# Expert blocks from two tables: 41 blocks start on batches 0 to 5, batch 7 is routed among them

## What is computed

```python
x = x + attention(layernorm(x))           # uv = silu(xn @ uv_w.T); rope; squared relu of the scores
h = layernorm(x)                          # then, in the expert part:
xn = layernorm(h) * gamma + beta
probs = softmax(xn @ Wr + br);  scores, idx = top_k(probs, 2)
full[e] = relu(xn @ W1[e] + b1[e]) @ W2[e] + b2[e]
c = einsum('ef,efh->eh', relu(b1), W2) + b2;   c_total = c.sum(axis=0)
out = x + h + sum_k scores[k] * (full[idx[k]] - c[idx[k]] + c_total)
```

## Time and profile before

| | us |
|---|---|
| three executions | 404.68, 396.47, 397.13 |
| median | 397.13 |
| the profiled execution, its own time | 393.24 |
| its span, first to last instruction | 390.9 |
| TensorE busy, of the span | 319.3 (82%) |
| VectorE, ScalarE, GpSimd busy | 263.2, 240.2, 194.6 |

### The profile page before, as it was taken

The page is one execution under the profiler, slowest core; times in us unless marked ns, Lnnn a source line. Parts: engine busy times, 40 slices in busy tenths (PEclk is TensorE's granted clock), DMA queues, the critical chain, the costliest instruction groups (busy, mean ns, idle before and its releaser), DMA issues.

```text
span 390.9 us, 7957 instructions
## 1 busy us (share of the span) xinstructions
PE 319.3 (82%) x2031; PEld 258.5 (66%) x2031; DVE 263.2 (67%) x923; ACT 240.2 (61%) x466; POOL 194.6 (50%) x194
## 2 busy tenths in 40 slices
PE   2639999999999999999750599999999998999100
PEld 1525565666566666665650499999999998999000
DVE  4593598878788887772648377667767665776082
ACT  2656698888979797935030467667777776775000
POOL 4132060477667766575577035455555545555252
PEclk9987999999999999999995599999999999999655
DMA  7882200010100000010113212222222222221296
GB/s 177 285 231 82 90 0 0 3 37 17 43 15 29 28 28 27 23 34 20 37 48 102 69 35 69 63 67 78 69 63 73 71 70 70 58 61 50 90 356 199
DMA packets 33647, 29.01 MB, mean 74 GB/s; under 512 B 5393, under 2 KB 28980, under 8 KB 33604
## 3 DMA queue, kind: packets, MB, share of 16 engines
q1 hardware_dynamic: 24770, 18.33, 16.5%
q0 software_dynamic: 4352, 8.47, 6.6%
q10 hardware_dynamic: 4482, 1.72, 1.6%
HBM read 17.34 MB, written 11.68 MB: 74 GB/s over the span
## 4 chain that ended last, share of the span: by engine, by line
PE 59%; DVE 11%; ACT 9%; DMA 7%; issue 6%; POOL 4%; SPq 2%; ACTq 0%; POOLq 0%; DVEq 0%
PE B_uv L793 14%; PE B_o L806 14%; PE B_o L704 7%; PE B_S L688 6%; PE B_o L713 4%; PE B_S L692 3%; DMA W2s<-y 3%; ACT xs L499 3%; POOL slots L427 2%; DVE go L937 2%; DMA y<-u,xb 2%; PE B_uv L671 2%; PE B_uv L647 2%; DMA xb<-slots 2%; SPq L363 1%
## 5 line engine op out<-in xcount | busy, mean ns | idle before, releaser
L447 POOL DMA_INDIRECT y<-u,xb x72 | 70.4, 978 | 79.6 <-ACT u L601 75.3
L427 POOL DMA_INDIRECT slots<-rows,pos x64 | 65.2, 1019 | 30.7 <-issue 17.0
L806 PE MATMUL B_o<-W2s,K 128*128 x576 | 76.9, 276 | 0.4 <-DVE K L1105 0.4
L806 PEld LDWEIGHTS B_o<-W2s,K 128*128 128x128 f32 x576 | 70.1, 192 | 0.9 <-issue 0.6
L704 PE MATMUL B_o<-K,v 128*128 128x512 f32 x128 | 59.0, 594 | 0.0
L1105 DVE TENSOR_SCALAR K<-B_uv,t 128x128 f32<-128x128 f32 x144 | 40.6, 345 | 25.4 <-PE B_uv L793 25.4
L596 ACT ACTIVATE t<-W1s 128x644 f32 x36 | 26.7, 741 | 34.6 <-DVE yd L1100 18.8
L793 PE MATMUL B_uv<-xbT,t 128*128 128x128 f32 x288 | 39.9, 284 | 0.0
L793 PEld LDWEIGHTS B_uv<-xbT,t 128*128 128x128 f32 x288 | 36.7, 200 | 0.2 <-issue 0.2
L704 PEld LDWEIGHTS B_o<-K,v 128*128 128x128 f32 x128 | 23.0, 190 | 20.3 <-issue 19.1
L688 PE MATMUL B_S<-qk 128*128 128x512 f32 x64 | 34.2, 618 | 0.0
(11 more groups left out here) (166 smaller groups left out, 660.1 us busy)
## 6 DMA issues: line engine op xcount, KB each, us to landing
xb<-slots SPq DMA_DIRECT2D x72, 65.0 KB, 1.8
x_all<-L_attn_x SPq DMA_DIRECT2D x8, 256.0 KB, 3.6
W1s<-L_ffn_W SPq DMA_DIRECT2D x1, 2048.0 KB, 13.6
W1s<-y SPq DMA_DIRECT2D x4, 512.0 KB, 5.7
W2s<-y SPq DMA_DIRECT2D x4, 512.0 KB, 9.5
out<-acc ACTq DMA_DIRECT2D x5, 256.0 KB, 5.3
y<-u,xb POOLq DMA_INDIRECT x72, 2.2
slots<-rows,pos POOLq DMA_INDIRECT x64, 2.4
```

The source lines that it names most:

```text
L427: pool.indirect_dma_start(out=slots, out_offset=bass.IndirectOffsetOnAxis(ap=pos[:, q % 2, c:c + 1], axis=0), in_=rows[:, q % 2, k, t, :], ...
L447: pool.indirect_dma_start(out=y2, out_offset=bass.IndirectOffsetOnAxis(ap=xb[:, k, D:D + 1].bitcast(u32), axis=0), in_=yb[:, k, :], in_off ...
L806: last = nc.tensor.matmul(B_y[(m - 1) % 2], hT[:, (m - 1) % 2, c * P:(c + 1) * P], W2s[:, bass.ds(w + c * D, D)], start=(c == 0), stop=(c ...
```

## The change

The list of blocks is cut in two. Batches 0 to 5 have 6144 rows in 8 regions; 41 of their 128-row blocks are full whatever the routing, and they get a table of their own (`table_a`) while stage 7, the attention of the last batch, still runs. The 30 blocks of a second table (`table_b`) hold the rest, first that of batches 0 to 5 (14 blocks), then that of batches 6 and 7. In particular:

- The pipeline ends with stage 7. `prefix(r)` stands ahead of `output(a)`, and `positions(r)` behind `ln2_stats(a)`, in the same stage.
- On TensorE the sum of the counts of batches 0 to 5 stands in the attention of batch 7 and the first two blocks are transposed ahead of `output(7)`. Batch 7's `transpose_xn`, `router`, `prefix` and the second count stand in the block loop behind blocks 3, 5, 8 and 10 (`XN_AT` to `COUNT_AT`), and the parts of the other engines at the places that answer to them; `table_b` is spread over seven blocks of VectorE from block 11.
- GpSimd scatters batch 6 ahead of all `put`s, and batch 7 in 8 pieces behind `put(12)` to `put(19)`. SP zeroes all 8 tails ahead of load 32.
- `expert_constants` is replaced. The relu is `max(h, -b1)`, one VectorE instruction of 512 elements in place of 4 of 128, and what it leaves out, `b1 @ W2`, is folded into the constant row. The sums over b1 are 32 products with 9 columns (`constant_rows`) in stage -1, one copy, 8 small products (`constants_of`) and two ACT evacuations (`evac_d`) in stage 0. They need masks in SBUF (`eye8`, `own`), which GpSimd makes at the program's start; `own` is 17 partitions of 1024 elements. W2 is loaded from ACT's queue, ahead of ACT's first computation, and b2 as 8 rows.
- `xb` and `yb` have 16 slots in place of 8, and there are 71 blocks in place of 72.
- The sums of batches 0 to 5 are made in the block loop from block 61, one instruction a block, from loads that begin when block 54 is written; batches 6 and 7 are loaded after the last block in halves of 256 KB, summed by VectorE alone and stored in halves.

```diff
@@ constants @@
-NSLOT = 8
-NBLK = -(-(ROWS * TOPK // P + NE - 1) // NSLOT) * NSLOT
+NSLOT = 16
+OLD = 6
+FULL = OLD * L * TOPK // P
+NA = FULL - (NE - 1)
+NB1 = ((FULL - NA) * P + NE * (P - 1)) // P
+NBLK = ROWS * TOPK // P + NE - 1
+NB = NBLK - NA
+XN_AT, ROUTER_AT, EXP_AT, PREFIX_AT, COUNT_AT = 3, 5, 7, 8, 10
+SCATTER_AT, TAILS_AT, ADD_AT = 12, 32, 61
@@ SP @@
+            sp.wait_ge(tabA_step, TABA)
+            sp.wait_ge(scattered[0], 16 * TOPK * T * (OLD // 2))
+            sp.wait_ge(scattered[1], 16 * TOPK * T * (OLD // 2))
+            for n in range(NBLK):
+                if n >= NSLOT:
                     sp.wait_ge(y_ready, n - NSLOT + 1)
+                    sp.wait_ge(blk_stored[n % NSLOT], 16 * (n // NSLOT))
+                if n == TAILS_AT:
+                    sp.wait_ge(tabB_step, TAIL_AT)
+                    zero_tails(sp, range(NE))
+                if n == NA:
+                    sp.wait_ge(tabB_step, TABB)
...
+                load_block(n)
             for k in range(NSLOT):
+                sp.wait_ge(blk_stored[k], puts_below(k, NA + NB1))
+            for b in range(OLD):
+                sp.dma_start(fin[b].rearrange("p t k d -> p t (k d)"), y2_rows(b)).then_inc(fin_loaded[b], 16)
@@ GpSimd @@
+            pool.memset(eye8[:, :, :], 0.0).then_inc(s_pool0, 1)
+            pool.memset(own[:, :, :], 0.0).then_inc(s_pool0, 1)
...
+            pool.affine_select(out=own[:, :, :], in_=own[:, :, :], compare_op=ALU.not_equal, fill=1.0,
+                               base=0, pattern=[[-1, NE], [0, P]], channel_multiplier=1).then_inc(s_pool0, 1)
+            pool.wait_ge(s_pool0, 20)
+            pool.affine_select(out=own[:, :, :], in_=own[:, :, :], compare_op=ALU.is_gt, fill=1.0,
+                               base=NE, pattern=[[0, NE], [0, P]], channel_multiplier=-1).then_inc(s_pool0, 1)
...
+                if a == BATCH - 1:
+                    scatter(r - 1, q)
+                    residual(a, q)
+            ln2_pow(BATCH - 1)
+            scatter(BATCH - 2, BATCH - 2)
+            for n in range(NBLK):
+                put(n)
+                if SCATTER_AT <= n < SCATTER_AT + TOPK * T:
+                    scatter_tile(BATCH - 1, BATCH - 1, n - SCATTER_AT)
@@ ACT @@
+            for n in range(NBLK + 2):
+                if n + 2 < NBLK:
+                    weights_of(n + 2)
+                if n >= 2:
+                    weighted(n - 2)
+                if n + 2 < NBLK:
+                    block_input(n + 2)
+                if n == XN_AT:
+                    evac_xnT(BATCH - 1)
+                    residual_of_ffn(BATCH - 1)
+                if n == EXP_AT:
+                    exps(BATCH - 1)
+                    copy_rows(BATCH - 1, BATCH - 1)
@@ PE @@
+            def constant_rows(experts):
+                if 0 in experts:
+                    te.wait_ge(s_ld_w2, 16)
+                    te.wait_ge(s_b1, 4)
+                for e in experts:
+                    for c in range(T):
+                        i = e * T + c
+                        last = nc.tensor.matmul(B_m[0:NE + 1, P:2 * P], b1_cols[:, i, :], W2s[:, i * D:(i + 1) * D],
+                                                start=(i == 0), stop=(i == NE * T - 1))
...
+                if r is not None:
+                    prefix(r)
+                if a == BATCH - 1:
+                    block_rows(0)
+                    block_rows(1)
                 if a is not None:
                     output(a)
@@ DVE @@
+            def hidden_relu(n):
+                dve.wait_ge(h_ps, n + 1)
+                after(dve, y_ps, n - 1)
+                if n == 0:
+                    dve.wait_ge(av_ps, BATCH)
+                tt(hT[:, n % 2, :].rearrange("p (c r) -> p c r", c=T), B_h[n % 2].rearrange("p (c r) -> p c r", c=T),
+                   W1c[n % 4][:, F + D:F + D + T].unsqueeze(2).broadcast_to([P, T, P]), ALU.max).then_inc(h_ready, 1)
...
-            for n, m in over_blocks(dve, 0):
-                if 0 <= m < NBLK:
-                    for c in range(T):
-                        last = ts(hT[:, m % 2, c * P:(c + 1) * P], B_h[m % 2][:, c * P:(c + 1) * P],
-                                  W1c[m % 4][:, F + D + c:F + D + c + 1], 0.0, ALU.add, ALU.max)
+            for n in range(NBLK + 2):
+                if 2 <= n:
+                    expert_sum(n - 2)
+                if n < NBLK:
+                    hidden_relu(n)
...
+                if ADD_AT <= n:
+                    add_choice(n - ADD_AT)
```

More of the change, by code:

```diff
@@ L267, in at, with loads_of, puts_below, y2_rows @@
                 return [b if 0 <= b < BATCH else None for b in (t + 2, t + 1, t, t - 1)] + [t]
-            for t in range(-2, BATCH + 1):
+            for t in range(-2, BATCH):
                 yield at(t)
[L271 to L289, removed]
+        def loads_of(n):
+            return 16 * (n // NSLOT + 1)
+        def puts_below(k, end):
+            return 16 * len(range(k, end, NSLOT))
+        def y2_rows(b):
+            return y2[b * L * TOPK:(b + 1) * L * TOPK, :].rearrange("(t p k) d -> p t (k d)", p=P, k=TOPK)
+        def out_rows(b):
+            return out[b, :, :].rearrange("(t p) d -> p t d", p=P)
         def zero_tails(eng, experts):
@@ new lines, in _ @@
+            for n in range(2):
+                weights_of(n)
+                block_input(n)
+            for n in range(NBLK + 2):
[11 more added lines that the diff above has]
+                    copy_rows(BATCH - 1, BATCH - 1)
@@ L747, in _ @@
                     scores(a)
-                if r is not None and a is not None and not (isinstance(r, int) and r == 0):
-                    prefix(r - 1)
                 if p is not None:
                     project_u(p, q + 1)
+                if a == 0:
+                    constants_of(0)
                 if p is not None and a is None:
@@ L763, in _ @@
                     project_v(p, q + 1)
+                    constant_rows(range(0, NE // 2))
                 if n is not None:
                     transpose_x(n)
+                if p is not None and a is None:
+                    constant_rows(range(NE // 2, NE))
                 if a is not None:
@@ new lines, in _ @@
+            for n in range(NBLK + 1):
+                if n < NBLK:
+                    hidden(n)
+                if n + 2 < NBLK:
+                    block_rows(n + 2)
+                if n >= 1:
+                    expert_out(n - 1)
+                if n == XN_AT:
+                    transpose_xn(BATCH - 1, BATCH - 1)
+                if n == ROUTER_AT:
+                    router(BATCH - 1)
+                if n == PREFIX_AT:
+                    prefix(BATCH - 1)
+                if n == COUNT_AT:
+                    count(1, BATCH)
@@ L1027, in _ @@
                     ln2_apply(r, q + 1)
-                if r is not None and a is not None and not (isinstance(r, int) and r == 0):
-                    positions(r - 1, q)
+                if a == BATCH - 1:
+                    table_a()
                 if p is not None:
```

497 lines of the change are left out of this document (302 added, 195 removed).

## The result

The changed kernel took 356.24 us (median of four executions, 355.8 to 356.79), the kernel before beside it 396.8 (four executions, 395.84 to 404.68): a ratio of 0.900 with an interval of 0.896 to 0.903, faster by 10%. The forecast of 365 was 8.8 us too high. The range of 356 to 375 holds the result by 0.24 us, which is luck; the range of 358 to 372 that went with the forecast itself doesn't hold it.

What follows compares the result with a forecast made beforehand. TensorE was taken to bound attention and blocks, but not start, entry and end. Span 390.9 + 4.6 + 1.3 − 24.4 − 0.6 − 12.9 = 358.9; plus 2.3, 361.2; times 1.010, 365 us. Range 356 to 375, its own 358 to 372.

Steps and rivals of the forecast that it cites:

- Start: Program start through stage 0: masks and wait +3.9, constant products net −1.1, constants_of and evac_d +1.8; together +4.6 us.
- Steady stages: Attention stages: moved prefix and positions leave 0.25 us a stage, +1.3 us over five stages, bounds −2.5 and +3.
- Entry: Between attention and blocks: block 0's second products start at 200.2 in place of 224.65, −24.4 us, bounds −26 and −20.
- The lower clock: In the entry to the blocks: TensorE idles some 3 us twice, so 1.5 us added, bounds 0 and 3.
- Blocks: Block loop: one block fewer −1.9, batch 7's pieces on TensorE and ScalarE, slot waits −1.4; together −0.6 us, bounds −2 and +5.
- half of it were waits for a slot, which 16 slots take away: −1.4: Block loop: of 2.8 us over the steady pace in 71 intervals, half were slot waits that 16 slots remove.
- End: Behind the last product: first sum after 7.2, sums 3.0, end 4.6, 14.8 in place of 27.7, −12.9 us.
- Rivals: Start costs more 371 us (0.13), batch 7 stalls blocks 372 (0.13), better (0.07), no gain (0.04), slower (0.03).
- The slow relu: Rival in the block loop: GpSimd holds VectorE's new relu; at 2.2 us the kernel takes over 405; chance 0.03.
- The good side: Rival at start and entry: clock stays and constants fill TensorE's idle time, both bounds good, 355 to 358 us; chance 0.07.

Runs made afterwards that it cites:

- e4: Changed kernel with the mask `own` (one memset, two selects) made behind ln1_pow(1) instead of at the start: 353.05 us against 356.2 beside it.
- e1: Changed kernel with batch 7's routing, second count, table_b and scatter moved ahead of the blocks: 384.49 us, in a disturbed group.
- e6: Changed kernel with GpSimd's residual(7) ahead of ln2_pow(6) and TensorE's output(7) ahead of the transpositions of blocks 0 and 1: 352.36 us.
- e8: Changed kernel with 8 slots and the 12 sums behind the block loop: 409.84 us, 395.84 with only the sums moved, both disturbed.
- e3: Changed kernel with loads of batches 0 to 5 also waiting for the last block and all sums behind the loop: span 404.3 us, disturbed group.
- e2b: Changed kernel with the 12 sums of batches 0 to 5 behind the block loop, their loads unmoved: 358.91 us beside 356.14.
- e7: Changed kernel with the relu again as four VectorE instructions of 128x128: 359.08 us.

## Why the prediction was right, and where it was off

**Start.** Right: 3.94, −1.30 and 2.32 us where +3.9, −1.1 and +1.8 were forecast. The large selects took 1.08 us each; 1.1 was taken between 0.29 and 2.3, a choice that came out well without a row behind it. VectorE started at 7.41, 7.4 was named. e4 shows that this is paid in full. The constant products took 3.66 us twice, 7.3 for 64 records, as the earlier trace rows had them; the clock stayed at 1.00 from 20 to 40 us, and `project_base(1)` took 0.96 us, not 1.65. (1.5 less 2.5 makes −1.0; the −1.1 in the sum is a slip of 0.1.) The 16 records of `constants_of` took 1.16 and 1.15 us, 0.144 each and not the 0.115 that was taken over. By the Trainium skill, TensorE: Matmul & The Clock Gate, section LDWEIGHTS, a weight load takes time by its columns; the trace agrees in direction, since with 9 columns in place of 128 a record of the loads took 0.091 us and not 0.190. But a record of the products stayed at 0.273 (0.275 before), and all 64 at 7.3 us, so the loads weren't what bounded them, and leaving that gain out of the sum was right.

**Steady stages.** +0.2 and not +1.3. Between 50 and 185 us TensorE waited 3.4 us in all for `go` before; after, 0.7 us for `go` and 1.8 ahead of `transpose_x`. The 0.25 us a stage that I left over from `positions` were all covered: stages last 20.6 us as before, not the 20.8 that was named.

**Entry.** −24.2 against −24.4. The chain that I named set it: the eighth scatter started at 191.20, the rows of block 0 came 5.28 us later (5.27 counted), and block 0's relu stood behind `positions(6)`. e1 shows that the larger part of the gain, some 20 us, is the routing and the table that now lie beside blocks. The lower clock, 1.5 us in the sum, cost `output(7)` 1.3. What I had not seen in it was `sel`, held by GpSimd. It didn't change the sum, since block 1's rows came only at 197.62, but e6 shows that with another order it can be taken out.

**Blocks.** The step "half of it were waits for a slot, which 16 slots take away: −1.4" is the term that was mis-sized: it was nearly all of them. From the start of the last four blocks' second products to the end of the last were 6.28 us (before) and 5.75 (after), 1.3 and 1.8 less than four times the pace, since first products run out there; taking this out, before lost 3.4 us inside the loop, and none of these losses came back. In the trace of before 3.1 of the 3.4 lie at five places where TensorE waited for a block's rows, and SP waited 50 times, 48.5 us in all, for a slot's block to be written. At three of the five only TensorE's weight loads show the wait (0.19 to 0.22 us, 2.4 in all five); the rows of the products show the other two, 1.4 us:

```profile
329.66 0.33 PE L801 MATMUL B_m<-ident,xb 128*128 128x128 f32 x1 [1.23 <-DMA xb<-slots]
...
356.75 0.33 PE L801 MATMUL B_m<-ident,xb 128*128 128x128 f32 x1 [0.21 <-DMA xb<-slots]
```

After, the only losses are those of batch 7: 44.01 for 22 intervals of 1.896, 2.3 us, where 2.7 were forecast. So −1.9 for the block, +2.3, −3.4 and −0.5 for the drain, −3.5. After, TensorE has no wait for rows in the loop, and in e8, with 8 slots, it has again; that the 16 slots alone took the 3.4 away no undisturbed run shows.

**End.** −14.1 against −12.9: first sum 7.9 us behind the last product (7.2), sums 3.25 (3.0), and 2.5 us from the last sum to the end, where I took 4.6. The stores are halved, and I scaled too little from the 5.6 of before. e3 and e2b put the gain on the early loads, with 11 us, and on the sums in the loop, with 2.7.

**Rivals.** None came. The slow relu is refuted by the rows: 0.678 to 0.694 us over 36 of them. e7 turns it round: the single relu is worth 2.9 us. The good side, 355 to 358, with a chance of 0.07, holds the measured time, but not for its reason: the clock and the fill were as in the forecast, and the surplus came from blocks, end and factor.

## What to carry to other kernels

Work that only prepares later rounds can be cut where it first has something complete, and the rest run beside the first rounds: of 20 us of routing 2.3 stayed. What stood ahead of the wait that all engines share was paid in full until a load bounded the start, so it should hold only what the first instructions need (3.1 us for the three instructions of one mask, 4.3 with all that could move). And a buffer count isn't only a backlog: it sets how far a queue can run ahead of a wait or of a batch of other DMAs in the same queue.

## Of the hardware, unexpected

An instruction of VectorE on 8 to 32 elements took 1.83 and 1.13 us in place of 0.17 and 0.19, and both ended within 0.1 us of the end of the GpSimd tensor operation beside them (193.49 and 193.45; 194.92 and 194.87). `pick`, which started with one of them, took its usual 0.23. By the Trainium skill, SBUF — State Buffer, section SBUF: two separate sides, the pair of ports is a lock held for a whole instruction, by whichever starts first, against a VectorE instruction with two SBUF inputs or in a two-port mode; for `sel`, with two SBUF inputs and a start 0.26 us behind GpSimd's, these rows agree. For `idf` that isn't shown: it has one SBUF input, the trace doesn't say whether it ran in a two-port mode, and by its row it started 0.52 us ahead of the operation with which it ended. Either way a short instruction on the path waited for a long one that isn't on it.

TensorE's clock was at its 1.2 GHz level after 3.5 us of idling ahead of `prefix(6)`, which cost `output(7)` 1.3 us: it took 3.36 us, and 2.05 in e6, where TensorE idled 0.92 us twice and the clock stayed at 2.4 GHz.
